# The same instructions on buffers that lie at other addresses: an attention and feed-forward kernel on one core

## The reference

```python
x = L0_attn_x                                   # (32, 512, 256)
x = x + ln(attn(ln(x), w_qkv, b_qkv, w_out, b_out))
x = x + ln(ffn(ln(x), W1, b1, W2, b2))
# attn: qkv = x @ w_qkv.T + b_qkv; 16 heads of 16; softmax(q k^T / 4 + mask) @ v; @ w_out.T + b_out
# mask: a key block of 128 is seen by its own query block, and block 0 sees and is seen by all
# ffn:  relu(x @ W1 + b1) @ W2 + b2, 1024 hidden values
```

## Time and profile before

| | us |
|---|---|
| timed runs | 2048.34, 2048.37, 2044.54; median 2048.34 |
| profiled execution | 2041.29 |
| its span, from the first to the last instruction | 2039.5 |
| TensorE busy | 1926.4 (94%) |
| VectorE busy | 1511.4 (74%) |
| ScalarE busy | 1406.0 (69%) |
| GpSimd busy | 741.6 (36%) |
| mean granted clock of TensorE | 0.978 of 2.4 GHz |

### The profile page before, as it was taken

One profiled execution on the slowest core, in us unless ns is written; L12 is line 12 of the kernel. 1 busy time (PEld: TensorE's weight loads), 2 busy tenths in 40 slices (PEclk: granted clock), 3 DMA queues, 4 the chain that ended last, 5 costly groups with the idle time before them and its releaser, 6 DMA issues. The chain is left out here.

```text
span 2039.5 us, 71012 instructions
## 1 busy us (share of the span) xinstructions
PE 1926.4 (94%) x27904; PEld 1575.7 (77%) x27904; DVE 1511.4 (74%) x2913; ACT 1406.0 (69%) x2343; POOL 741.6 (36%) x910
## 2 busy tenths in 40 slices
PE   5789999999999999999999999999999999999985
PEld 3458888777878877888777788787788887778775
DVE  4687777787777778778777777777777777876731
ACT  1457767777776777776677777677777677776763
POOL 3113333334333334433343433333433333343343
PEclk7799999999999999999999999999999999999997
DMA  5333434433333433333343333343334344333200
GB/s 144 74 70 80 89 77 86 85 76 82 81 81 79 93 79 80 79 81 81 82 85 80 79 77 81 80 94 78 77 77 86 76 87 85 78 81 69 56 28 17
DMA packets 132815, 160.60 MB, mean 79 GB/s; under 512 B 29408, under 2 KB 82400, under 8 KB 132576
## 3 DMA queue, kind: packets, MB, share of 16 engines
q1 hardware_dynamic: 130544, 154.13, 35.7%
q10 hardware_dynamic: 2032, 2.69, 0.4%
HBM read 38.21 MB, written 17.83 MB: 27 GB/s over the span
## 5 line engine op out<-in xcount | busy, mean ns | idle before, releaser
L817 DVE TENSOR_REDUCE max_bias<-p_pair 128x4 f32<-128x1024 f32 (+1 forms) x640 | 772.8, 1222 | 262.0 <-PE p_pair L571 139.8
L742 ACT ACTIVATE probs<-p_pair 128x1024 f32<-128x1024 f32 x640 | 634.8, 1026 | 208.4 <-PE p_pair L568 127.6
L964 POOL TENSOR_TENSOR h_lo<-h_f,h_hi 128x512 fp32r<-128x512 f32 x256 | 329.7, 1288 | 507.5 <-ACT h_hi L774 507.5
L571 PE MATMUL p_pair<-stack 49*128 49x256 f32 (+1 forms) x3072 | 319.6, 306 | 39.5 <-DVE max_bias L817 22.7
L774 ACT ACTIVATE h_f<-p_pair,b_s 128x256 f32<-128x256 f32 x512 | 248.8, 486 | 133.1 <-PE p_pair L598 133.1
L571 PEld LDWEIGHTS p_pair<-stack 49*128 49x128 f32 (+1 forms) x3072 | 226.9, 188 | 126.7 <-DVE max_bias L817 59.8
L598 PE MATMUL p_pair<-w_hi,h_hi 64*128 64x256 f32 x2048 | 309.4, 279 | 5.0 <-ACT h_hi L774 2.5
L598 PE MATMUL p_pair<-x_hi,w_hi 64*128 64x256 f32 (+1 forms) x2560 | 302.1, 306 | 9.6 <-DVE x_lo L827 5.2
L598 PE MATMUL p_pair<-w_hi,h_lo 64*128 64x256 f32 x2048 | 305.7, 275 | 0.0
L598 PE MATMUL p_pair<-w_lo,h_hi 64*128 64x256 f32 x2048 | 305.5, 275 | 0.0
L598 PE MATMUL p_pair<-x_hi,w_lo 64*128 64x256 f32 (+1 forms) x2560 | 297.7, 302 | 0.0
(11 more groups left out here) (81 smaller groups left out, 2792.9 us busy)
## 6 DMA issues: line engine op xcount, KB each, us to landing
stack<-qk SPq DMA_DIRECT2D x1536, 64.0 KB, 2.3
xr<-x SPq DMA_DIRECT2D x32, 512.0 KB, 4.2
out<-yf SPq DMA_DIRECT2D x64, 256.0 KB, 2.2
xa<-x SPq DMA_DIRECT2D x31, 512.0 KB, 3.8
shift_rows<-max_t SPq DMA_DIRECT2D x128, 8.0 KB, 1.4
stack<-shift_rows SPq DMA_DIRECT2D x128, 8.0 KB
probs<-w_qkv_t SPq DMA_DIRECT2D x2, 384.0 KB, 5.5
ya<-w ACTq DMA_DIRECT2D x1, 512.0 KB, 8.2
```

Of the source, the lines that this page charges most:

```text
L571: last = nc.tensor.matmul(dst[:, j, col:col + HALF].rearrange("p (a n) -> p a n", a=2), stack[r, stationary, at, kb * P:(kb + 1) * P], two ...
L742: nc.scalar.activation(probs[:, prob_slot(quad, c), :, :], banks("scores", n)[:, :, :], ACT.Exp, scale=SCALE).then_inc(exp_done, 1)
L817: nc.vector.tensor_reduce(dst, src, axis=AX.X, op=ALU.max, negate=True).then_inc(red_done, 1)
L964: nc.gpsimd.tensor_tensor(h_parts[1][:, m:m + 2, :], h_f[:, n % 2, :, :], h_parts[0][:, m:m + 2, :].bitcast(F32), ALU.subtract).then_inc(h ...
```

## The change

No instruction is added, removed or moved: the lists of all five engines are the same, and all line numbers behind L346 are one higher. What changes is the order of the `sb` calls and the shape of one buffer. The small buffers (`bqk_s`, `b1_s`, `minus_half`, `eps`, `den`), `max_bias`, `max_t` and `values` move behind `yf`. `max_bias` gets rows of 320 in place of 272 values, and the biases `bv_s` and `bo_s` in it begin at value 64 in place of 16. The 128 columns of it that `max_t` transposes hold 16 maxima, then before 112 values of a bias, and now 48 unused ones and 64 of a bias; only the 16 maxima are read from the result.

```diff
         w_hi, w_lo = sb("w_hi", [P, WCOLS], F32R), sb("w_lo", [P, WCOLS], F32R)
         ident = sb("ident", [P, P])
-        bqk_s, b1_s = sb("bqk_s", [P, 4]), sb("b1_s", [P, KF])
         b2_s = sb("b2_s", [P, D])
-        minus_half, eps = sb("minus_half", [P, KB]), sb("eps", [P, KB])
         xa = sb("xa", [P, KB, D])
...
         stack = sb("stack", [P, 2, PAIRS, L], F32R)
-
-        max_bias = sb("max_bias", [P, 2, 4 * KB + D])
-        neg_max = [max_bias[:, j, 0:4 * KB].rearrange("p (s j k) -> p s j k", s=2, j=2) for j in range(2)]
-        bv_s, bo_s = [max_bias[:, j, 4 * KB:4 * KB + D] for j in range(2)]
-        max_t = sb("max_t", [4 * KB, P], F32R)
         shift = nc.dram_tensor("shift_rows", [2, 4 * KB, P], F32, kind="Internal").ap()
-        values = sb("values", [P, KB, H * VW + 32 - VW])
 
         probs = sb("probs", [P, CH + 2, 2, L])
         o_t = sb("o_t", [P, L])
-        den = sb("den", [P, 2, 2 * KB])
         o_n = sb("o_n", [P, KB, D])
...
         yf = sb("yf", [P, KB, D])
+
+        max_bias = sb("max_bias", [P, 2, 5 * P // 2])
+        neg_max = [max_bias[:, j, 0:4 * KB].rearrange("p (s j k) -> p s j k", s=2, j=2) for j in range(2)]
+        bv_s, bo_s = [max_bias[:, j, P // 2:P // 2 + D] for j in range(2)]
+        max_t = sb("max_t", [4 * KB, P], F32R)
+        values = sb("values", [P, KB, H * VW + 32 - VW])
+        bqk_s, b1_s = sb("bqk_s", [P, 4]), sb("b1_s", [P, KF])
+        minus_half, eps = sb("minus_half", [P, KB]), sb("eps", [P, KB])
+        den = sb("den", [P, 2, 2 * KB])
```

## The result

| | us |
|---|---|
| kernel before, median of 5 timed runs | 2048.37 (2044.54 to 2051.61) |
| changed kernel, median of 5 | 2061.41 (2059.80 to 2063.84) |
| ratio, 95% interval | 1.0062 (1.0045 to 1.0079) |
| span of the profiled execution | 2039.5 before, 2059.6 changed |

The account below looks back on a forecast made before the run. The prediction took TensorE's pace per matmul to bound the kernel. All its terms were taken at 0, giving no effect (chance 0.60) and 2047 us, a little under the median of before, with a range of 2036 to 2060 us.

Parts of the forecast that it names:

- What bounds the kernel: Whole kernel: TensorE's pace through 27,904 matmuls bounds it, busy 1926.4 of 2039.5 us; 113 us missing placed in end slices.
- Step (a): TensorE's operands: the 3% spread between matmul units is a matter of place in the order, not address; taken at 0.
- no unit of `f1` at 1.37 left: Profile after, units of `f1`: named as a sign that the forecast was wrong towards slower.
- The slower rival at the matmuls: `f2`, `f1`, `op`: reads at 192 are the fast ones; 24 us in full, half taken, 12 us, 2059 us; chance 0.12.
- The faster rival: `v`, `qk`, matmuls on `stack`: a read from residue 0 is slow; 14 us gained, 2034 us; chance 0.16.
- (b): VectorE, ScalarE, GpSimd: 2 to 3% between residues 0 and 192, at most 4.4 us on VectorE; taken at 0.
- (c): `max_bias`: its halves move to residue 128 and rows grow to 1280 bytes; reductions and transposition unchanged, 0.
- (d): Small buffers (statistics, `den`, biases, `eps`) at other multiples of 32: a few times 0.02 us, taken as 0.
- Step (e): DMA, loads of `stack` from `qk` leaving residue 0: between nothing and 10% of 2.3 us; taken at 0.
- The rival of the growing loads: Loads of `stack`: 10% more, 0.23 us, waited for once in each of 32 batches; 7 us, 2054 us; chance 0.06.
- The change does not do what it says: Buffers at 128, not 0, modulo 256: nothing gained, first four lose theirs; counted inside no effect and the two slower rivals.

Follow-up runs that it names:

- the run that moved the first group alone: Kernel before with 128 bytes ahead of `xa` and of `max_bias`: `xa`, `x1`, `qk`, `stack` go from residue 0 to 128; 2044.94 us, 0.9993.
- only the last group moved: Kernel before with 192 bytes ahead of `o_n`: the ten buffers at residue 192 go to 128; 2063.86 us, 1.0082.
- the odd multiples of 32: Changed kernel with pads: from `w`, modulo 128, `x1` and `o2` at +32, `x2` and `h` at +96; 2058.29 us, 1.0059.
- the split of `stack`: Kernel with `w` at 128, rest at 192, plus 64 unused bytes behind each half of `stack`, moving all buffers behind it to 64; 2048.61 us, 1.0017.
- The run meant to show it: Changed kernel with 64 bytes between `h_hi` and `h_lo`, so `h_lo` at 192, `h_hi` and `w` at 128; 2060.4 us in one run.

## Why the prediction was wrong

**What bounds the kernel** was right: TensorE's pace per matmul, and the whole of a change in it reached the span (20.9 us of busy time, 20.1 of span). The reading of the slices was loose: three slices at the start and two at the end are below 9, and 53 of the 113 us without work lie in the stretch from 64 to 1900 us. No term hangs on it.

**Step (a) failed.** It put the price of TensorE's operands at 0; it was 20 us of span, 0.60 us a turn. I had the right pair in hand, `v` against `op`, with the right size, 3%. I set it aside because two units of `f1` on the same buffers showed the same two paces, and concluded that the pace was a matter of place and not of address. The conclusion doesn't follow. Place chooses between the paces that a layout allows; the layout says which there are. At +64 a step of 113 to 114 ns is possible; in the changed kernel, at 0, no unit of `f1` took less than 1.42 us, 118.5 ns a step, and one sign that I had named for a slower kernel, no unit of `f1` at 1.37 left, came true. A 3% spread with fixed addresses hid a 3 to 5% effect of the addresses. My grouping was also of the wrong kind: I sorted buffers by their own residue, and the run with everything at 192 shows that 192 in place of 128 for all changes nothing. In a table of stationary against moving residue the same rows would have read: `f2` and `op` at +64, `f1` at -64, `v` at 128, and after the change all at 0, a distance that no dense product of the kernel before had. That was the point at which the trace could not bound the cost, and I had bounded it by rows that were all on one side.

**The slower rival at the matmuls** (0.12, 2059 us) came nearest, by a wrong mechanism: not that reads at 192 are fast. Its full price of 24 us would have been close to the 20 of the span; I halved it on the two units of `f1`. But the dense units that carry the cost are `f2`'s, and most of them were at the fast pace (the first unit in 20 of 28 turns, the second in all, the fourth in 22), while the price per unit was larger than mine, 0.13 us in place of 0.08. The range ended at 2060 because of that half; the time was 2061.41.

**The faster rival** is refuted by the run that moved the first group alone: 2044.94 us, with `v` no faster than before. (Its 14 us off 2047 make 2033, not 2034.)

**Steps (b), (c) and (d) held.** The maxima still take 1225 ns in the median, and VectorE and GpSimd are busy within 1.3 us of before. The normalization still takes 409 ns on `xr` and 396 on `xa`, to the nanosecond, though both now stand at 128; so their residue doesn't part them, as I had said could be seen:

```profile
L917 DVE TENSOR_SCALAR xr<-xr,mv_ln,rstd_ln 128x256 f32<-128x256 f32 x128 | 46.9, 409 | 16.8 <-ACT x_old L784 12.0 <-POOL rstd_ln L960 4.8
...
L917 DVE TENSOR_SCALAR xa<-xa,mv_ln,rstd_ln 128x256 f32<-128x256 f32 x128 | 45.3, 396 | 0.5 <-POOL rstd_ln L960 0.5
```

**Step (e) held for the time and not for the work.** The loads of `stack` land 2.3 us after issue in all kernels. But the DMA engines are busier wherever `qk` and `stack` stand off a multiple of 256. The row of the queue (packets, MB, share of 16 engines) in the kernel before, and in the run that moved the first group alone, whose span is 1.0 us shorter:

```profile
q1 hardware_dynamic: 130544, 154.13, 35.7%
```

```profile
q1 hardware_dynamic: 130544, 154.13, 38.6%
```

That is 8% more of the queue's time for the same packets. It is 35.4% in the two runs that leave `qk` and `stack` at a multiple of 256 (only the last group moved, and the odd multiples of 32), and 38.1 to 39.3% in all eleven kernels that do not. The Trainium skill (DMA: Bandwidth & Descriptors, How a descriptor splits into AXI transactions) says that a read that does not start at a multiple of 256 bytes fetches from the multiple below it; by its table a 2 KB row that starts 128 past one takes 68 beats for 64, an estimate of 6%. The trace agrees in the direction, with 8%. It cost nothing here: in the steady stretch TensorE waited for `stack` 2.4 us in the changed kernel and 2.8 us in the run that moved the first group alone, 1.9 us before, and the time of that run did not move. The rival of the growing loads was right that the transfers cost the DMA engines more and wrong that they land later.

**"The change does not do what it says"** is half true. Its buffers are 128 past a multiple of 256, but that is harmless: what harms is that they all share one residue, and with a base at 0 they would share it as well. This last is inferred from the runs at 128 and at 192, not run.

## What to carry to other kernels

Where TensorE is the bound and back-to-back matmuls load a new stationary operand each time, look at the distance between the addresses of the two operands of each product before aligning anything; equal alignment for all was among the slowest layouts here (1.0062 and 1.0082 of the kernel before; only `h` at a distance of 128 was as slow, 1.0104), and 64 bytes of padding took it back. When the same instruction shows two paces on the same buffers, that does not clear the buffers: tabulate the paces by the relation of its operands, and price a relation that the trace has not seen as unknown on both sides. And an edit that moves buffers for one reason moves the distances of all those behind it, as the split of `stack` did.

## What the runs showed of the hardware that was not expected

- A step of two 64x256 float32r matmuls on 64 partitions each, with a new stationary operand every time, takes 113.3 to 120.0 ns in the second unit of `f2` and the second of three `f1` in a row, and which of these depends on the addresses of its two SBUF operands. By distance modulo 256, `f2`: 114 ns at +64, 117 at -32, 118 at -64, 119 at +96, 120 at 128, 119 to 120 at 0. `f1`: 113 at +64, 113 or 118 at -64, 118 at +96, 120 at 0 and at -96. In all these runs but the one with everything at 192, `w` stood at 128.
- At equal residues some units have a rigid pace (the fourth of `f2` took 2.880 us in each of 28 turns), though not all: `v`'s second took 1.42 to 1.44. At others a unit can settle at either of two values as a whole, so `f2`'s first unit took 2.74 or 2.84 us from turn to turn without any change of address.
- Three of the four units of `pv`, with 32-column stationary operands in rows of 1148 bytes, took 2.29 us in every layout.
- That the extra time comes from the read of the moving operand meeting the load of the next stationary one is my reading of it. The run meant to show it left it open, and why the sign counts is open too, as is whether the period is 256 bytes for every product.
